# A two-layer Mamba-2 block with a mixture of experts: one written-out program per kind of unit, work moved between VectorE, ScalarE and GpSimd

## The reference

```python
for i in range(2):                       # layers
    res = h
    h = _layernorm(h, ln_w[i], ln_b[i])
    # in_proj to z (512), xBC (640), dt (8 heads); dt = softplus(dt + dt_bias)
    # xBC = silu(causal 4-tap convolution); xh (8 heads of 64), B, C (64 each)
    # state = exp(dt*A) * state + (dt * x) B^T ;  y = state C + D * x
    # y = y * silu(z);  y = y * rsqrt(mean(y^2) + eps) * rms_w;  h = y @ out_w.T + res
x = _layernorm(x + h)
# router: top 2 of 8 experts, softmax of the two; each expert 256 -> 2*1024 -> 256, silu gate
x = _layernorm(x + sum of the two experts' weighted results)
```

## Time and profile before

| | |
|---|---|
| three timed runs | 1635.63 us median (1634.18 to 1643.03) |
| the profiled execution | 1643.5 us, its span 1641.6 us |
| busy, of the span | PE 1353.8 us (82%), DVE 1160.7 (71%), ACT 741.4 (45%), POOL 780.7 (48%) |
| mean granted TensorE clock | 0.918 of full speed |
| issues of 512 KB of `step_rows` by SP | 64, 4.5 us each from issue to landing (median) |

### The profile page before, as it was taken

One profiled execution on the slowest core, in us unless ns is written; L12 is line 12 of the kernel. 1 busy time (PEld: TensorE's weight loads), 2 busy tenths in 40 slices (PEclk: granted clock), 3 DMA queues, 4 the chain that ended last, 5 costly groups with the idle time before them and its releaser, 6 DMA issues.

```text
span 1641.6 us, 40122 instructions
## 1 busy us (share of the span) xinstructions
PE 1353.8 (82%) x13198; PEld 1044.9 (64%) x13199; DVE 1160.7 (71%) x2658; ACT 741.4 (45%) x1682; POOL 780.7 (48%) x665
## 2 busy tenths in 40 slices
PE   2788888888887887887877529999999999999970
PEld 1355555556555554555544428999999999998960
DVE  4788988888988778688787656656565656565552
ACT  2554455554445424434432305445444444544443
POOL 1245555554654355455466626334132615072875
PEclk9799999999999888888887659999999999999995
DMA  4322323323332121330222132230313213123656
GB/s 138 103 65 78 116 93 112 97 70 103 103 116 73 58 97 53 98 93 30 97 93 106 60 128 90 89 111 29 106 32 109 83 58 106 32 80 98 103 104 147
DMA packets 97991, 145.88 MB, mean 89 GB/s; under 512 B 13504, under 2 KB 81856, under 8 KB 97792
## 3 DMA queue, kind: packets, MB, share of 16 engines
q1 hardware_dynamic: 79776, 98.51, 19.0%
q0 software_dynamic: 18144, 46.51, 10.9%
HBM read 103.19 MB, written 41.80 MB: 88 GB/s over the span
## 4 chain that ended last, share of the span: by engine, by line
PE 51%; DVE 16%; issue 15%; POOL 11%; ACT 2%; DMA 2%; SPq 1%; POOLq 1%; DVEq 0%; ACTq 0%
PE pe L814 11%; PE pa L814 11%; PE py L826 10%; DVE arena L1178 4%; PE pa L601 4%; PE py L690 3%; DVE arena L1215 3%; POOL arena L1855 3%; PE pm L721 3%; PE pa L593 3%; POOL arena L1784 2%; POOL arena L1774 1%; DVE arena L1223 1%; PE pt L792 1%; PE pz L696 1%
## 5 line engine op out<-in xcount | busy, mean ns | idle before, releaser
L814 PE MATMUL pe<-arena 128*128 128x128 f16 x3456 | 218.8, 219 | 6.4 <-issue 6.4
L814 PE MATMUL pa<-arena 128*128 128x128 f16 x3456 | 218.5, 219 | 0.0
L814 PEld LDWEIGHTS pe<-arena 128*128 128x128 f16 x3456 | 201.7, 97 | 13.3 <-issue 12.8
L826 PE MATMUL py<-arena 128*128 x1728 | 200.5, 273 | 2.8 <-DVE arena L1605 1.6
L814 PEld LDWEIGHTS pa<-arena 128*128 128x128 f16 x3456 | 200.9, 97 | 0.0
L1061 ACT ACTIVATE arena<-pe,arena 128x128 f32<-128x128 f32 x576 | 164.3, 373 | 79.9 <-PE pe L814 78.0
L1178 DVE SCALAR_TENSOR_TENSOR arena<-pa,arena 128x511 f32<-128x511 f32 (+2 forms) x240 | 178.2, 745 | 15.9 <-ACT arena L877 9.9
L1577 DVE SCALAR_TENSOR_TENSOR pm<-pa,arena 128x128 f32<-128x128 f32 x288 | 81.7, 352 | 139.3 <-ACT arena L1061 130.2
L826 PEld LDWEIGHTS py<-arena 128*128 128x128 f16 x1728 | 165.6, 98 | 21.7 <-issue 3.6
L1784 POOL TENSOR_TENSOR arena<-arena 128x512 f32<-128x512 f32 x64 | 81.3, 1270 | 202.2 <-DVE arena L1242 201.9
L721 PE MATMUL pm<-arena 128*128 128x256 f16 x768 | 114.3, 308 | 49.4 <-DVE arena L1151 49.4
(11 more groups left out here) (219 smaller groups left out, 2480.6 us busy)
## 6 DMA issues: line engine op xcount, KB each, us to landing
arena<-step_rows SPq DMA_DIRECT2D x64, 512.0 KB, 4.5
arena<-in_w_exp POOLq DMA_DIRECT2D x32, 768.0 KB, 4.8
arena<-queue SPq DMA_DIRECT2D x75, 129.5 KB
answer<-arena SPq DMA_DIRECT2D x72, 128.0 KB
arena<-in_x SPq DMA_DIRECT2D x16, 512.0 KB, 5.8
answer<-zeros SPq DMA_DIRECT2D x10, 512.0 KB, 4.7
arena<-h SPq DMA_DIRECT2D x9, 512.0 KB, 5.2
h<-arena SPq DMA_DIRECT2D x8, 512.0 KB, 2.9
```

Source lines behind the costliest of these rows:

```text
L814: ins = pe.matmul(bank[:, f * P:(f + 1) * P], w_split[:, p, hl, d * 2 * FF + col:d * 2 * FF + col + P], x[:, r, d, :], start=(n == 0), sto ...
L826: ins = pe.matmul(py[:, 0:D], a[:, b, f, :], part(p, hl, W1N + f * D, D), start=(half == 0 and n == 0), stop=(half == 1 and n == len(passe ...
```

## The change

`schedule` calls six programs instead of three: `prologue`, `first` (unit 0), `plain` (1 to 8), `routed` (9 to 14), `final` (15) and `epilogue`, each written out for each of the four engines with an order of its own. The pieces are smaller: `chunk_b` becomes `chunk_y` and `chunk_s`, the C·B product leaves `chunk_a` as `chunk_cb`, the squares leave `chunk_c`, the states leave `chunk_b2`, GpSimd's `operands` become `x_dt`, `x_w`, `x_d` and `old_state`. Three things change engines. Both normalisations (`ln_apply`, `s3_apply`, now `x1_apply`) go from VectorE to ScalarE as scale times x plus bias; for the bias VectorE writes the negated mean and GpSimd multiplies it by the power. The first state's copy goes from VectorE to ScalarE. The low halves `u_low` go from VectorE to GpSimd. `end_a` goes to GpSimd, its division into the squares' scale. `end_b` stands in mid-unit in `plain` and early in `routed`, not at a unit's start; `end_b` before had the place right behind `dt_first`. In `plain` the `scatter_before` calls, left out below, do nothing. Lines taken out are not shown in the new programs.

```diff
-def schedule(eng, body, prologue, epilogue):
+def schedule(eng, prologue, first, plain, routed, final, epilogue):
 
     prologue(Step(-1, -1, 0, 1, FIRST, 0))
-    body(Step(0, 0, 0, 0, PLAIN, 7, first=True))
+    first(Step(0, 0, 0, 0, PLAIN, 7, first=True))
     with eng.Fori(0, 3) as i:
         for r in range(2):
...
+            def chunk_cb(c):
+
+                q, n, k = c.q, c.n, c.k
+                tk = slice(k * P, (k + 1) * P)
+                if k == 0:
+                    pe.wait_ge(xc_done, 5 * c.u + 1)
                 at_least(pe, m_done, n)
                 pe.matmul(CBT, bT[0:DS, q, tk], cT[0:DS, q, tk], start=True, stop=True).then_inc(cb_full, 1)
...
+            def chunk_s(c):
+
+                q, k, kq = c.q, c.k, c.kq
+                pe.wait_ge(xw_ready, 3 * c.u + k + 1)
+                at_least(pe, z_free, c.u6 + 2 * k)
+                pe.wait_ge(bs_ready, c.u + 1)
+                pe.matmul(pz[0:DS, :], bs[:, q, k, :], xw[:, kq].rearrange("p h d -> p (h d)"),
+                          start=True, stop=True).then_inc(z_full, 1)
...
+            def plain(st):
+                c = [Chunk(st, k) for k in range(NK + 1)]
+                chunk_a(c[1])
+                do_fills(st, ["dt"])
+                chunk_cb(c[1])
+                do_fills(st, ["c4"])
+                do_fills(st, ["c0"])
+                chunk_s(c[0])
+                chunk_y(c[0])
+                chunk_z(c[1])
+                steps(st.u + 1, 1 - st.q)
+                do_fills(st, ["c1"])
+                chunk_c(c[0])
+                chunk_s(c[1])
+                chunk_y(c[1])
+                do_fills(st, ["c2"])
+                chunk_a(c[2])
+                chunk_z(c[2])
+                chunk_d(c[0])
+                chunk_cb(c[2])
+                do_fills(st, ["c3"])
+                chunk_s(c[2])
+                turn_b(st.u + 1, 1 - st.q, c[0].n + 1)
+                chunk_c(c[1])
+                do_fills(st, ["z0"])
+                chunk_y(c[2])
+                chunk_d(c[1])
+                chunk_a(c[3])
+                chunk_cb(c[3])
+                do_fills(st, ["z1"])
+                do_fills(st, ["z2"])
+                do_fills(st, ["ln0"])
+                chunk_c(c[2])
+                chunk_z(c[3])
+                chunk_y(c[3])
+                chunk_a(c[4])
+                do_fills(st, ["ln1"])
+                chunk_d(c[2])
+                chunk_c(c[3])
+                chunk_cb(c[4])
+                do_fills(st, ["z3"])
+                chunk_d(c[3])
...
+            def routed(st):
...
+                chunk_cb(c[3])
+                do_fills(st, ["z0"])
+                do_fills(st, ["lg"])
+                chunk_z(c[3])
+                chunk_c(c[2])
+                do_fills(st, ["z1"])
+                chunk_y(c[3])
+                do_fills(st, ["z2"])
+                do_fills(st, ["rk"])
+                chunk_a(c[4])
+                do_fills(st, ["ln0"])
+                chunk_d(c[2])
+                chunk_c(c[3])
+                do_fills(st, ["ln1"])
+                do_fills(st, ["z3"])
+                chunk_cb(c[4])
+                chunk_d(c[3])
...
+            def ln_apply(w, wq):
+                e.wait_ge(ln_rs, w + 1)
+                for k in range(NK):
+                    ins = e.activation(hln[:, wq, k, :], hln[:, wq, k, :], ACT.Identity, scale=rs[:, k:k + 1],
+                                       bias=nb[:, k:k + 1])
+                ins.then_inc(ln_done, 1)
+
+            def x1_apply(st):
+                wq = 1 - st.q
+                e.wait_ge(r_rs, st.u - NB)
+
+                before = st.h - 1 if wq == 1 else st.h
+                e.wait_ge(stored[wq], 16 * before + 16)
+                e.wait_ge(scattered[wq], 128 * (before - 4) + 16)
+                e.sem_inc(hop, 1)
+                for k in range(NK):
+                    ins = e.activation(x1b[:, wq, k, 0:D], ob[:, wq, k, :], ACT.Identity, scale=rrs[:, k:k + 1],
+                                       bias=rnb[:, k:k + 1])
+                ins.then_inc(x1_ready, 1)
+
+            def first_state(c):
+                e.wait_ge(z_full, c.u6 + 1)
+                e.activation(state[0:DS, 0].rearrange("p h d -> p (h d)"), pz[0:DS, :], ACT.Copy).then_inc(z_free, 1)
...
+            def plain(st):
+                c = [Chunk(st, k) for k in range(NK + 1)]
+                softplus(st)
+                chunk_a(c[1])
+                conv_first(st, "c4")
+                conv_first(st, "c0")
+                first_state(c[0])
+                chunk_c(c[0])
+                steps(st)
+                conv_silu(st, "c4")
+                conv_first(st, "c1")
+                conv_silu(st, "c0")
+                chunk_a(c[2])
+                conv_first(st, "c2")
+                conv_silu(st, "c1")
+                squares(c[0])
+                chunk_d(c[0])
+                conv_silu(st, "c2")
+                conv_first(st, "c3")
+                squares(c[1])
+                chunk_c(c[1])
                 b_rows(st)
+                z_silu(st, 0)
+                ln_apply(st.u + 2, st.q)
+                chunk_d(c[1])
+                chunk_a(c[3])
+                z_silu(st, 1)
+                squares(c[2])
+                conv_silu(st, "c3")
+                chunk_c(c[2])
+                z_silu(st, 2)
+                ln_out(st, "ln0")
+                chunk_a(c[4])
+                ln_out(st, "ln1")
+                chunk_d(c[2])
+                chunk_c(c[3])
+                squares(c[3])
+                chunk_d(c[3])
+                z_silu(st, 3)
...
+                at_least(dve, ln_rs, w)
+                dve.tensor_scalar(nm, mv[:, :, 0], -1.0, None, ALU.mult)
                 dve.tensor_scalar(ve, mv[:, :, 1], EPS, None, ALU.add).then_inc(ln_var, 1)
-
-            def ln_apply(w, wq):
-                dve.wait_ge(ln_rs, w + 1)
-                for k in range(NK):
-                    ins = dve.tensor_scalar(hln[:, wq, k, :], hln[:, wq, k, :], mv[:, k, 0:1], rs[:, k:k + 1],
-                                            ALU.subtract, ALU.mult)
-                ins.then_inc(ln_done, 1)
...
+            def plain(st):
+                c = [Chunk(st, k) for k in range(NK + 1)]
                 scan(c[1])
+                dt_first(st)
+                chunk_mix(c[1])
+                ch1 = Chain(dve, c_dve2, S1_LINKS, st.u + 1)
+                dt_last(st, ch1)
+                scan(c[2])
+                taps(st, "c4", ch1)
+                chunk_b2(c[0])
+                chunk_b1(c[1])
+                taps(st, "c0", ch1)
+                weigh(st)
+                end_b(st)
                 g_low(c[0])
                 chunk_b2(c[1])
+                next_state(c[1])
+                taps(st, "c1", ch1)
+                chunk_b1(c[2])
+                taps(st, "c2", ch1)
+                chunk_mix(c[2])
+                ln_stats(st.u + 2, st.h + 1, st.q)
                 g_low(c[1])
+                taps(st, "c3", ch1)
+                ch1.close()
                 chunk_b2(c[2])
+                next_state(c[2])
                 scan(c[3])
                 chunk_mix(c[3])
                 chunk_b1(c[3])
+                g_low(c[2])
                 chunk_b2(c[3])
+                scan(c[4])
                 g_low(c[3])
+                chunk_mix(c[4])
...
+            def routed(st):
+                c = [Chunk(st, k) for k in range(NK + 1)]
+                scan(c[1])
+                dt_first(st)
+                chunk_mix(c[1])
+                ch1 = Chain(dve, c_dve2, S1_LINKS, st.u + 1)
+                dt_last(st, ch1)
+                taps(st, "c4", ch1)
+                chunk_b2(c[0])
+                end_b(st)
+                taps(st, "c0", ch1)
+                g_low(c[0])
+                chunk_b1(c[1])
+                ch3 = s3_stats(st)
+                chunk_b2(c[1])
+                scan(c[2])
+                next_state(c[1])
+                weigh(st)
+                taps(st, "c1", ch1)
+                chunk_b1(c[2])
+                g_low(c[1])
+                taps(st, "c2", ch1)
+                chunk_mix(c[2])
+                taps(st, "c3", ch1)
+                ch1.close()
+                scan(c[3])
+                chunk_b2(c[2])
+                next_state(c[2])
+                ln_stats(st.u + 2, st.h + 1, st.q)
+                chunk_mix(c[3])
+                chunk_b1(c[3])
+                s3_top(st, ch3)
+                g_low(c[2])
+                chunk_b2(c[3])
+                s3_place(st, ch3)
+                scan(c[4])
+                g_low(c[3])
+                chunk_mix(c[4])
...
+            def u_low(w, wq, st, name):
+
+                (bank, before), d = st.fill(name), int(name[2])
+                pool.wait_ge(a_free[bank], before + 1)
+                pool.tensor_tensor(uT[:, wq, 1, d, :], uf[:, d, :], uT[:, wq, 0, d, :], ALU.subtract
+                                   ).then_inc(ul_ready, 1)
...
```

(83 more changed lines are left out.)

706 lines of the change are left out of this document (439 added, 267 removed).

## The result

The changed kernel takes **1539.07 us** (median of 4 runs, 1535.93 to 1541.8) against 1637.72 for the kernel before, a ratio of 0.9394 (95% interval 0.936 to 0.9429). The forecast was 1490 us. The time lies inside the whole range (1460 to 1555), but outside the forecast's own (1465 to 1515): of 148 us forecast, 99 came.

The account below looks back on a forecast made before the run. No engine was full; handing over in a fixed order bound the units. Prologue -2, first unit -7.6, plain -47, routed -79, last -11, tail -1: together -148, from 1635.6 to 1488, rounded 1490 us; range 1460 to 1555.

Parts of the forecast that it names:

- the walk's 41: Plain units: stepping through the new instruction lists with durations from the old profile, a unit closes at 41 us.
- 42.5 with its additions: Plain units: 41 us plus 0.5 for waits and 1 for `end_b` meeting `add_xd`; 48.4 to 42.5 us, -47 for eight.
- the tail: Stretch from last unit to the experts, 48.8 us: normalisation 0.7 slower, one low part less, together -1 us.
- ScalarE's 2.1 us: Normalisations moved to ScalarE: four activations of 128x256 with scale and bias per row cost 2.1 us.
- GpSimd's 1.16: Low halves moved to GpSimd: 1.16 us each.
- two rivals, 1542 and 1550: `end_b` slowed by GpSimd in full, 1542 us, 11%; the orders not holding, only VectorE's time gained, 1550 us, 11%.
- The second: Rival: the orders do not hold, only VectorE's time is gained, plain -4.4, routed -6.9, 1550 us; 11%.
- Forecast 49.5 us each: Routed units: 47 us plus the plain units' additions doubled; 62.7 to 49.5 us, -79 for six.
- It closes at 47: Routed units: stepping through the new lists, with `s3_place` and `scan` at 5.5 us before `g_low(c3)`, closes at 47 us.
- `end_b` meets GpSimd in full: Rival: each of four `end_b` instructions waits, 5.2 us instead of 1.7 in 15 units, +52, 1542 us; 11%.
- the clock, taken as full: TensorE's granted clock: fuller queues keep it up, near 1.00; a rival with a low clock, slower than before, had 4%.

Follow-up runs that it names:

- e4: The changed kernel with plain and routed units back in the earlier kernel's orders on all four engines, the new split of work kept: 1650.6 us, 0.6% slower than before.
- e9: e2 with `end_b` of the routed units moved behind `g_low(c0)`: 1501.7 us.
- e3: The changed kernel with the edits of e1 and e2 together, routed units alone: 1507.4 us.
- e2: The hold: changed kernel, routed units, GpSimd's last two scatters behind `gated(c3)`, then GpSimd waits for the end of `s3_place` before `x_w`: 1508.4 us.
- e1: The changed kernel with `end_b` of the routed units moved from behind `chunk_b2(c0)` to right behind `dt_first`: 1542.3 us.
- e8: The changed kernel with both normalisations of the plain and routed units applied on VectorE again, not on ScalarE: 1619.1 us.

## Why the prediction was right or wrong

**Right: what bounded, and the plain units.** The waits at the hand-overs fell with the new orders (186.0 to 68.9 and 60.8 to 7.0 us), while the relief in the old orders gave nothing (e4, with its reservation). Plain units gave 53.6 us (forecast 47); the walk's 41 was nearer than 42.5 with its additions. `end_b` met one GpSimd instruction there, 1.0 us, as assumed. First unit 6.6 (7.6) and last unit 11.8 (11; 36.1 us from `end_b` to `end_b`) were right, and the tail is the same 48.8 us. ScalarE's 2.1 us and GpSimd's 1.16 came as read.

**Luck in the range.** 1539 lies inside 1460 to 1555 because that range was drawn around two rivals, 1542 and 1550, and neither is what happened. The second was also mis-added: it took 6.9 us of relief in a routed unit where the prediction's own lines give 7.9, so it stood 6 us too high.

**Wrong: one term, the routed units.** Forecast 49.5 us each, -79 for six; measured 57.1 on average in units 9 to 13, and -33.6 for the six. That is 45.4 of the 45.7 us by which the whole gain fell short of the sum; the other misses (-6.6 plain, +1.0 first, +2.7 start, +3.0 experts and smaller ones) cancel. The step was "It closes at 47": the walk took `s3_place` and `scan` as 5.5 us in front of `g_low(c3)`, where they are 9.4, and `s3_top` as 2.7, where it is 4.4. These durations came from a kernel in which GpSimd's arithmetic ended in time: VectorE (unit 10 of before)

```profile
618.42 0.18 DVE L1320 TENSOR_TENSOR arena<-arena 128x32 f32<-128x32 f32 x1
618.53 1.00 DVE L1321 TENSOR_TENSOR arena<-arena 128x4 f32<-128x4 f32 x1
```

and GpSimd, arithmetic and then a scatter:

```profile
618.45 1.06 POOL L1765 TENSOR_TENSOR arena<-arena 128x512 f32<-128x512 f32 x1
619.67 1.00 POOL L1746 DMA_INDIRECT queue<-arena  x1 [0.16 <-issue]
```

One instruction of four columns was caught there, at 1.00 us: the row that would have warned me, and I had read only the sum. I priced the contention for `end_b` alone, the wide instruction that the change moved. But it has no width: an instruction of four columns waits for the whole GpSimd instruction too, and `s3_place` has six that were caught (the copy at 596.66 in part). With GpSimd out of the way and `end_b` moved (e9) units 9 to 13 take 49.3 us on average, near the forecast's 49.5, and the two units of e3 that kept a clock of 0.96 take 47.9 and 47.8, near the walk's 47. So the walk of the orders held about as far as it can be tested, and durations that it had taken as fixed did not. The second thing it had wrong is the clock, taken as full.

**The rival that fits the number and not the cause.** "`end_b` meets GpSimd in full" had 5.2 us and 1542; measured 5.16 in routed units, 2.68 in plain ones, and 1539. A reader of the first and the last number would call it confirmed. But the 3.5 us were to be lost in 15 units, eight of which lost 1.0, and the plain units gave more than forecast; the agreement of the totals is luck. What the long `end_b` cost shows in e9 against e2: it is 3.2 us shorter there, and the unit 1.4. e1 can't say, since it puts `end_b` on another chain.

**The clock.** It is 1.00 in plain units, as forecast, and 0.89 in routed ones, not full: TensorE waited up to 5.1 us for `g_low(c3)`. It went to 0.94 with the hold, and was 0.83 in e4 and 0.81 in e8. In the stretches looked at, a wait of TensorE came first: in unit 10 of the changed kernel it ran at half clock from 604 to 614 us, beginning within the wait for `g_low(c3)`. But the low clock adds to what the wait costs where TensorE has no pause behind it, as in e1 and e3.

**Not settled.** The part from the first expert product on has the same code and took 3.0 us more, and 2 to 6 more in all twelve experiments (668.6 to 673.3, against 666.9), always against one profile of before. No run tells why.

## What to carry to other kernels

Walk a new order with durations that belong to the new neighbours: mark every short VectorE instruction with SBUF operands that stands in a chain, and ask what GpSimd does at that moment. Then let GpSimd do its DMA issues there, with no arithmetic close behind, and its arithmetic under scans and PSUM evictions. When a stall is removed by moving its instruction and the time stays, look at what the instruction now stands in front of, and at the clock behind it, before calling the stall harmless. Test a relief and an order together as well as apart, and treat the places of the moved work as part of the test.

## What the runs showed of the hardware

A short VectorE instruction caught beside GpSimd arithmetic ends within 0.1 us of that one's end: 1.05 us for 4 columns (0.16 alone), 2.56 for 32 columns behind two of them (0.19 alone). Caught were TENSOR_TENSOR and SCALAR_TENSOR_TENSOR with both inputs in SBUF, and TENSOR_SCALAR, COPY and CAST with one. Not caught beside such arithmetic were TENSOR_REDUCE (0.18), and in e2 the scan (2.33) and the eviction (0.67), each with one input in PSUM.

Scatters are milder, but not free. In e2 the products of `s3_place` beside a scatter took 0.16 to 0.19 us, while its two casts took up to 0.41 together, from 0.24 in the unit shown, and ended when the scatter did. And an instruction that starts beside a scatter with arithmetic close behind is held until that arithmetic ends, as this one of `s3_top` in the changed kernel:

```profile
591.47 1.87 DVE L1537 TENSOR_TENSOR arena<-arena 128x4 f32<-128x4 f32 x1
```

```profile
591.05 0.96 POOL L2078 DMA_INDIRECT queue<-arena  x1 [0.30 <-issue]
592.03 1.28 POOL L2117 TENSOR_TENSOR arena<-arena 128x512 f32<-128x512 f32 x1
```

The same happened to the long `a_s` of e3 and to `end_b`, one instruction of which started 0.45 us into a scatter and took 2.93 us. Starts on GpSimd are rough in these profiles, so whether the hold begins before the arithmetic does is open.

The Trainium skill (SBUF — State Buffer, Who interferes with whom) has just these classes: two SBUF inputs meet GpSimd's reads, copy, cast and `tensor_scalar` can take both ports, a reduction never does. The rows agree with it for each class; that the price does not shrink with the operand is what I had not carried into the sum.
